# A linear-attention and expert block on one core: the attended product in 256 columns, and its halves picked when the output is turned back

## The reference

```
attn  = einsum('bihd,bjhd->bhij', qb, kb) * causal
intra = einsum('bhij,bjhe->bihe', attn, vb)
inter = einsum('bihd,bhde->bihe', qb, Sst)
Sst   = Sst + einsum('bjhd,bjhe->bhde', kb, vb)
o     = intra + inter
```

## Time and profile before

| | |
|---|---|
| median of 3 runs | 1153.3 us (1145.38 to 1154.67) |
| the profiled execution | 1154.31 us, its span 1152.6 us |
| mean granted clock of TensorE | 0.969 |
| PE busy | 1030.0 us (89%) |
| DVE busy | 903.6 us (78%) |
| ACT busy | 665.7 us (58%) |
| POOL busy | 512.3 us (44%) |

### The profile page before, as it was taken

One profiled execution on the slowest core, in us unless ns is written; L12 is line 12 of the kernel. 1 busy time (PEld: TensorE's weight loads), 2 busy tenths in 40 slices (PEclk: granted clock), 3 DMA queues, 4 the chain that ended last, 5 costly groups with the idle time before them and its releaser, 6 DMA issues.

```text
span 1152.6 us, 23833 instructions
## 1 busy us (share of the span) xinstructions
PE 1030.0 (89%) x7766; PEld 721.8 (63%) x7766; DVE 903.6 (78%) x2107; ACT 665.7 (58%) x1651; POOL 512.3 (44%) x477
## 2 busy tenths in 40 slices
PE   6776888899998789999998989989998999899997
PEld 4554565566665556666665657657776677677774
DVE  5885677899985667887798877898889887877764
ACT  2543455556655566767675755646675665555563
POOL 2074154503334542132212237858886554466551
PEclk9997899999998999999999999989999999999997
DMA  9997133323333332222222233232533052214320
GB/s 301 354 399 106 56 123 108 124 76 102 107 104 101 97 94 74 69 77 74 64 72 63 56 108 111 74 101 70 139 103 101 12 158 83 80 54 115 104 71 18
DMA packets 87047, 124.00 MB, mean 108 GB/s; under 512 B 11280, under 2 KB 70160, under 8 KB 82832
## 3 DMA queue, kind: packets, MB, share of 16 engines
q1 hardware_dynamic: 76688, 97.30, 28.1%
q0 software_dynamic: 10240, 25.18, 7.6%
HBM read 71.32 MB, written 51.13 MB: 106 GB/s over the span
## 4 chain that ended last, share of the span: by engine, by line
PE 50%; DVE 27%; ACT 9%; issue 8%; another core or an unknown queue 5%; DMA 0%; DVEq 0%; POOL 0%; SPq 0%; ACTq 0%; POOLq 0%
PE bank L1433 6%; PE wide L1457 6%; PE bank L1719 5%; PE bank L1517 5%; PE bank L1709 5%; PE wide L1709 5%; DVE epp L1795 4%; PE bank L1501 3%; DVE kvw L1802 3%; DVE att L1559 2%; PE bank L1509 2%; PE bank L1420 2%; PE bank L1447 1%; ACT epp L1770 1%
## 5 line engine op out<-in xcount | busy, mean ns | idle before, releaser
L1672 POOL TENSOR_TENSOR kvw<-kvw,hq 128x512 f32<-128x512 f32 x128 | 171.3, 1338 | 150.7 <-ACT kvw L1762 150.4
L261 POOL DMA_INDIRECT routed_rows<-hq,idxs x128 | 131.2, 1025 | 232.5 <-DVE att L1559 98.7
L921 POOL DMA_INDIRECT gst<-attended_rows,idxs x128 | 135.2, 1057 | 203.4 <-DVE att L1559 100.2
L1559 DVE SCALAR_TENSOR_TENSOR att<-reach,endrel,wide 128x1024 f32<-128x1024 f32 x152 | 194.4, 1279 | 22.3 <-PE wide L1457 12.6
L1795 DVE TENSOR_TENSOR epp<-kvw,epp 128x512 fp32r<-128x512 f32 x160 | 142.9, 893 | 77.7 <-ACT epp L1770 75.6
L1719 PE MATMUL bank<-epp,w2p 128*128 128x512 f32 x480 | 162.7, 448 | 8.3 <-DVE epp L1795 8.1
L1770 ACT ACTIVATE epp<-kvw 128x512 fp32r<-128x512 f32 x160 | 100.8, 630 | 94.6 <-DVE kvw L1802 89.9
L1709 PE MATMUL bank<-hp,w1p 128*128 128x512 f32 x480 | 140.3, 401 | 0.0
L1709 PE MATMUL wide<-hp,w3p 128*128 128x512 f32 x480 | 138.5, 397 | 0.0
L1433 PE MATMUL bank<-kvw,turned 128*128 x304 | 131.1, 513 | 5.7 <-ACT turned L1321 2.7
L1762 ACT ACTIVATE kvw<-bank 128x512 f32<-128x512 f32 x160 | 94.7, 592 | 57.0 <-PE wide L1709 55.9
(11 more groups left out here) (265 smaller groups left out, 1876.6 us busy)
## 6 DMA issues: line engine op xcount, KB each, us to landing
hq<-weight_rows SPq DMA_DIRECT2D x16, 2048.0 KB
rows<-routed_rows SPq DMA_DIRECT2D x76, 256.0 KB
routed_rows<-zero SPq DMA_DIRECT2D x2, 7168.0 KB
attended_rows<-ob SPq DMA_DIRECT2D x76, 128.0 KB
routed_rows<-zero SPq DMA_DIRECT2D x1, 5120.0 KB, 19.2
out<-fin SPq DMA_DIRECT2D x16, 256.0 KB, 2.4
routed_rows<-hq,idxs POOLq DMA_INDIRECT x128
gst<-attended_rows,idxs POOLq DMA_INDIRECT x128
```

Of the source, the lines that this page charges most:

```text
L261: pool.indirect_dma_start(hs[s], bass.IndirectOffsetOnAxis(idxs[:, t, k:k + 1], 0), hq[:, t, :], None, bounds_check=BLOCKS[s] * P - 1, oob ...
L921: pool.indirect_dma_start(gst[:, u, k, :], None, orow[s], bass.IndirectOffsetOnAxis(idxs[:, t, k % TOPA:k % TOPA + 1], 0), bounds_check=BL ...
L1559: dve.scalar_tensor_tensor(out=att[:, n % 2, :, :], in0=reach[:, :, :].rearrange("p a c -> p (a c)").unsqueeze(1) .to_broadcast([P, 4, 2 * ...
L1672: pool.tensor_tensor(g, g, rows_of(1 - b % 2, n, n + 1), ALU.mult).then_inc(s_eu, 1)
```

## The change

v is stored without zeros, 128 columns a block. attend is four products of 256 columns, one a strip: the stationary operand is the v of both heads (32 columns), the moving one is the scores of both. A strip's rows then have, in the first 128 columns, the even head's scores times the v of both heads, and in the last 128 the odd head's scores times both. In each half 16 of the 32 rows are wanted. A block's output takes 256 columns of bank 2 in place of 128, the pair's the whole bank. carried writes state times q into both halves, by a moving operand that repeats q. keep_outputs copies 512 columns. turn_outputs multiplies each half by an identity in which only the rows of the even, or of the odd, heads are one, and adds the two: four ordinary products with two results, in place of two transposes. GpSimd makes these half identities where it cleared vx before; for that it waits for s_xT to reach NB, which is the turning of the last sequence in the routing part. ScalarE's wait for the zeros is gone.

```diff
@@ routing_gpsimd
-            pool.memset(vx[:, :, :, :], 0.0).then_inc(s_vx, 1)
+            pool.wait_ge(s_xT, NB)
+            for par in range(2):
+                ins = pool.tensor_scalar(halves[:, par, :], ident[:, :], parity[:, par:par + 1], None, ALU.mult)
+            ins.then_inc(s_hm, 1)
@@ tiles
-        vx = tb("vx", [P, 6, H, 2 * DK])
+        vx = tb("vx", [P, 6, P])
+        halves = tb("halves", [P, 2, P])
-        oTs = tb("oTs", [P, 2 * P])
+        oTs = tb("oTs", [P, 2, 2, P])
@@ attention_scalar
-                act.activation(vx[:, n % 6, :, 0:DK], bank[1][:, P:2 * P].rearrange("q (h d) -> q h d", d=DK),
-                               ACT.Copy).then_inc(s_ve, 1)
+                act.activation(vx[:, n % 6, :], bank[1][:, P:2 * P], ACT.Copy).then_inc(s_ve, 1)
...
-                act.activation(oTs[:, :], bank[2][:, 0:2 * P], ACT.Copy).then_inc(s_oc, 1)
+                act.activation(oTs[:, :, :, :].rearrange("p a h t -> p (a h t)"), bank[2][:, :],
+                               ACT.Copy).then_inc(s_oc, 1)
...
-            act.wait_ge(s_vx, 1)
@@ attention_tensor, turn_outputs
+                if g == 0:
+                    pe.wait_ge(s_hm, 1)
                 for a in range(2):
-                    mm = pe.transpose(bank[0][:, (2 + a) * P:(3 + a) * P], oTs[:, a * P:(a + 1) * P], ident[:, :])
+                    for par in range(2):
+                        mm = pe.matmul(bank[0][:, (2 + a) * P:(3 + a) * P], oTs[:, a, par, :], halves[:, par, :],
+                                       start=(par == 0), stop=(par == 1))
                 mm.then_inc(s_ot, 1)
@@ states
-                pe.matmul(bank[1][:, 3 * P:4 * P], km[:, m % 4, :], vx[:, m % 6, :, 0:DK], start=True,
+                pe.matmul(bank[1][:, 3 * P:4 * P], km[:, m % 4, :], vx[:, m % 6, :], start=True,
@@ carried
-                pe.matmul(bank[2][:, n % 2 * P:(n % 2 + 1) * P], sm[:, (n + 3) % 4, :], qm[:, n % 4, :],
+                pe.matmul(bank[2][:, n % 2 * 2 * P:(n % 2 + 1) * 2 * P].rearrange("p (h t) -> p h t", h=2),
+                          sm[:, (n + 3) % 4, :], qm[:, n % 4, :].unsqueeze(1).to_broadcast([P, 2, P]),
                           start=(n % 2 == 0), stop=True, skip_group_check=True)
@@ attend
-                v = vx[:, n % 6, :, :].rearrange("q h c -> q (h c)")
-                for par in range(2):
-                    for p in range(4):
-                        mm = pe.matmul(bank[2][32 * p:32 * p + 32, n % 2 * P:(n % 2 + 1) * P],
-                                       v[:, (4 * p + par) * DK:(4 * p + par + 2) * DK],
-                                       att[:, n % 2, p, par * P:(par + 1) * P], start=False, stop=True,
-                                       skip_group_check=True)
+                for p in range(4):
+                    mm = pe.matmul(bank[2][32 * p:32 * p + 32, n % 2 * 2 * P:(n % 2 + 1) * 2 * P],
+                                   vx[:, n % 6, 32 * p:32 * p + 32], att[:, n % 2, p, :], start=False, stop=True,
+                                   skip_group_check=True)
```

More of the change, by code:

```diff
@@ L1209, in adaln_block @@
         k1s = tb("k1s", [P, 2, P])
-        vx = tb("vx", [P, 6, H, 2 * DK])
+        att = tb("att", [P, 2, 4, 2 * P])
+        vx = tb("vx", [P, 6, P])
+        halves = tb("halves", [P, 2, P])
         turned = tb("turned", [P, 3, 2, 2, P])
         qx = tb("qx", [P, 2, 2, 2, P])
-        att = tb("att", [P, 2, 4, 2 * P])
         sh = tb("sh", [P, 2, P])
@@ L1225, in adaln_block @@
         s_vz = sem("first_state_zero")
-        s_vx = sem("zeros_between")
+        s_hm = sem("halves_of_identity")
         s_kf = sem("k_features")
```

## The result

| | before | changed |
|---|---|---|
| median | 1152.2 us (4 runs) | 1189.5 us (4 runs; 1185.55 to 1197.1) |
| ratio of the runs | 1 | 1.0345, 95% interval 1.0299 to 1.0391 |
| the profiled execution | 1154.3 us, span 1152.6 | 1197.1 us, span 1195.4 |
| granted clock, mean | 0.969 | 0.971 |

The forecast was 1219 us (5.7% slower), with a range of 1188 to 1247. The direction holds and the time lies at the range's very lower end: 37 us were added by the medians, 40 by the ratio and 43 in the profiled executions, not 66.

A forecast was written before the change was run, and what follows sets the result against it. The prediction took TensorE to bound the attention part: 83.6 us of added work + 6 for the longer copy - 24 swallowed by waits = +65.6 us, giving 1219 us (5.7% slower), range 1188 to 1247 us.

The forecast's parts named there:

- What bounds the kernel: Attention part: TensorE busy 501.15 of 552.00 us, so its added work adds time; routing and expert stages keep their work.
- The work on TensorE, +83.6 us: Attention blocks: carried product +33.4 us and back-turn +50.2 us, 1.10 us a pair; unbroken pair from 5.95 to 7.05 us.
- Rival D: Back-turn: an ordinary product costs four transposes, adding 1.54 us a pair, 67 us more, 1286 us in all; chance 0.02.
- The attended product, "I take no change": Attended product in each block: 16 records become 8, streaming stays 0.43 us, total stays 0.57 us; bounds -21 to +11 us.
- My best case: Attended product: nothing but the streaming is left, 0.43 in place of 0.57 us in 152 blocks, -21 us.
- Rival E: Attended product bound by its count of loads and matmuls, halved to 0.285 us, -43 us; 1145 us in all; chance 0.05.
- The waits, -24 us: TensorE's waits in the attention part, 48.1 us: half swallow added work; ends 0 and -48 us.
- The copy of 512 columns, +6 us: ScalarE's output copy before the back-turn: 0.21 us longer each, delaying TensorE; ends 0 and 11 us.
- Rival C: Attention part: TensorE's waits swallow all they can, 83.6 - 48.1 = +35.5 us, 1189 us in all; chance 0.13.
- GpSimd, ScalarE's dropped wait, SP: Off the path: GpSimd some 11 us later but still 19 us early, ScalarE's dropped wait gives nothing, SP's queue unmoved.

The follow-up runs named there:

- a_split: The changed kernel with its attended product cut again into eight products of 128 columns, 16 records a block; 1.0496 of the kernel before.
- b_both: The kernel before with only TensorE's added work: carried product written twice, back-turn as four ordinary products with the whole identity; 1.0465 of the kernel before.
- a_attend_only: The changed kernel with only the attended product's new form kept (128-column carried product, 256-column copy, two transposes), odd heads' outputs left out; 0.9933 of the kernel before.
- a_copy256: The changed kernel with the copy of the outputs over 256 columns only, all four back-turn products reading these; 1.035 of the kernel before.
- a_pick: The changed kernel with wanted halves picked by ScalarE and VectorE on the way out of bank 2, back-turn two transposes again; 1.0448 of the kernel before.

## Why the prediction was right or wrong, point by point

- **What bounds the kernel**: right. TensorE in the attention part; the routing and expert parts kept their length.
- **The work on TensorE, +83.6 us**: right, term by term (0.43, 0.89, 7.08 us in the chain). Rival D, four transposes' time for a product, is out.
- **The attended product, "I take no change"**: this step failed. Its time on the array did not change, as argued. But I had priced it by its own duration alone and not by when the engine behind it hears of its end. By a_split and the changed kernel the 8 records are worth 16 to 17 us, by b_both and the changed kernel 12 to 14 us, by a_attend_only, where VectorE takes over, 8 us. My best case had 21 us for it, but from shorter streaming, which didn't come. The hint stood in rows that I had read: the copy's waits in the earlier trace rows are for a copy that takes 0.38 us, with 0.42 and 0.65 us of TensorE's work ahead of the back-turn. I had put its lateness down to ScalarE's queue, which is busy in 9 of the 61 us.
- **Rival E** named the count of loads and matmuls as its mechanism and excluded it by the streaming time. The count does matter, at a third of E's price and by the signal, not by the array. Against 84 us more of work it does not decide the sign.
- **The waits, -24 us**: near, for part of the reason. b_both swallows 30 us of its added work by the ratio. TensorE's listed waits fell by 22.1 us in it, from 48.1 to 26.0: 11.4 at the masked scores, as argued, 6.0 before the back-turn, the rest scattered. In its profiled execution the stretch from the first back-turn to the last grew by 51.1 us, so some 10 of the 84 us are in no list (83.6 - 51.1 - 22.1); where they went is open. In the changed kernel the waits are 21.0 us, where I forecast some 25, but 8.0 of them are for the masked scores, which I had as nearly gone.
- **The copy of 512 columns, +6 us**: wrong in size; a_copy256 shows no cost (1.035 against 1.0345 and 1.0357), and the waits for it are the same with the short copy.
- **Together**: 83.6 - 30 - 14 + 0 = 40 us. This closes by construction, as both subtractions come from b_both; the 16 to 17 us of a_split are the separate witness for the 14. Rival C had the time right (1189 us) and the reason wrong: the waits did not swallow all they could, 21.0 us of them are left. That 1189.5 us still lies in my range is partly luck: its lower end, 1188, stands for all waits swallowed and no gain from the attended product, which is not what happened.
- **GpSimd, ScalarE's dropped wait, SP**: right; nothing came of them.

**Open**: why TensorE's signals are late. Shown is that the lateness at the attended product goes with the number of records in the four column strips (16 against 8, with the same operands and columns), that it falls when TensorE gets other work, and that the signals of the products right behind are late too. Whether the loads or the matmuls count, whether the product ends late or only its signal comes late, and what holds it, was not tried. That the 16 to 17 us of a_split go through this lateness is argued from the sums (41 us against 22) and TensorE's wait for the copy (24.8 us against 4.7), not tried apart.

## What to carry to other kernels

Price work that is added to the engine that bounds a stretch at its full duration, then take off only the waits that another engine's finished work would cover: here 84 us cost 54, and the next 67 cost 58. A product's price is also when the next engine hears of its end: fewer and longer products in the column strips gave 12 to 17 us here with the same time in the chain. Where a form saves that way but needs its results sorted out afterwards, the sorting must not cost the bounding engine more (84 us here), nor be handed to an engine that runs its queue in order and has long work ahead of it (a_pick).

## What the runs showed of the hardware

- A product of 128x32 weights by 256 columns in four column strips (8 records) takes 0.57 us in the chain, like twice as many of 128 columns (16 records). But the copy that waits for it starts after the modelled end by 22 us in sum over 76 pairs in the first form and 61 in the second, and by 41 when the first is only cut into 16 records (a_split). 57 of the 61 us lie before TensorE's signal comes.
- Signals of TensorE can come well after the modelled end of their product, for several products in a row: in the kernel before by 1.6, 1.9 and 1.7 us for three in sequence from 416.70 us on.
- An ordinary fp32 product of 128 by 128 columns costs twice a transpose: 8 records in 0.89 us, 2 in 0.22.
- A moving operand that repeats 128 columns by an access pattern takes twice the 0.22 us of 128 columns, 0.43 us; the repetition makes it no cheaper.
